# Weight spectra: the row transform of a 64x64 plane as products on the two row halves of TensorE, with copies of two PSUM banks

## The chip, the cores and the metric

One NeuronCore of a Trainium2 chip runs the whole program in one launch. The metric is the device time of that launch in microseconds (us), the median of several runs. All inputs and outputs are float32 in HBM.

## The reference, cut to what matters

The input `x` (16 images, 32 channels, 64x64 pixels) goes through four layers; each adds a convolution of its group-normalised input to `x`. The change concerns the fourth, which convolves with 32x32 filters of 64x64 pixels through Fourier transforms:

```python
x_f = jnp.fft.rfft2(x)
k_f = jnp.fft.rfft2(weights)          # weights: (32, 32, 64, 64)
out_f = jnp.einsum('bchw,ochw->bohw', x_f, k_f)
out = jnp.fft.irfft2(out_f, s=(H, W))
```

`k_f`, the weight spectra, depend on no other layer. The kernel computes them first of all, in a stage of its own, and keeps them in HBM until the fourth layer.

## The kernel before, in words

**The tiles.** `kernel_spectra_stage` (L270) goes over 8 tiles, in a loop of 4 rounds with two tiles each (`p` = 0 and 1, with their own source buffers `ks_src`). A tile has 128 planes of 64x64 pixels on the 128 partitions, 4096 pixels each: 8 chunks of 512.

**The steps of a tile.** All four are TensorE work in float32, written out in `forward_products` (L361).

1. `turn(j)` (L373) transposes chunk j, four blocks of 128x128 against the identity (L378), into PSUM bank `j % 4`. VectorE copies the bank to `ks_tt`, one of four buffers (L435, in `copy_turned`). A block of 128 turned partitions holds two image rows of 64 pixels, one in partitions 0 to 63, one in 64 to 127.
2. `rows(j)` (L381) is the transform along the rows: four products (L385), each with a 128x128 block of `ks_tt` as stationary operand (loaded into the array by a weight load) and the constant `ks_fw` as moving operand. `ks_fw` is block diagonal: twice the same 64x64 matrix, zeros elsewhere, so half of each product multiplies by zero. The result goes to bank `4 + j % 4`. ScalarE copies each bank back over `ks_src` (L447, in `copy_rows`).
3. `turn_columns(s)` (L398) transposes again (L404), into banks 0 to 3, which VectorE copies to `ks_cols` (L438). In odd tiles VectorE takes statistics of `x` in between (L204).
4. `columns(s)` (L407) is the transform along the columns (L412); for s = 0 four products more with 32 columns of weights (L417). ScalarE copies the results to `ks_spec` (L352), which its queue then sends to HBM (L357).

**What sets the order.** The order on TensorE is written out: three chunks are turned ahead (`AHEAD`), then turn(j+3) and rows(j) alternate, for j = 5 to 7 only rows are left; the columns go the same way. TensorE's queue waits for `turned_read` (VectorE has copied a turned bank) and `made_read` (ScalarE has emptied a result bank); the first `turn_columns` waits for all row copies of the tile, since it reads pixels of every chunk. VectorE waits for `turned` and, from chunk 4 on, for `made`, because the buffer `ks_tt` of chunk j-4 must have been used by its row product. `made` counts 16 per tile: 8 chunks and 8 column steps. SyncE's queue loads the next tiles (L303) and `x` (L305), two tiles ahead.

A float32 product runs as two weight loads and two matmul instructions, so that the 256 row products are 512 records of each kind; a transpose is one of each.

Of the kernel before, what the change touches and what calls it, by code (L numbers as in the profile page):

```python
# [19 lines left out]
F32 = mybir.dt.float32  # L20
# [7 lines left out]
P = 128  # L28
# [127 lines left out]
class Program:  # L156


    def __init__(self, nc, ctx, ins, out):
        self.nc, self.ins, self.out, self.names = nc, ins, out, set()  # L160
        self.ctx = ctx
        self.X = self.sb(ctx, "X", [P, Q, PIX])
        self.ident = self.sb(ctx, "ident", [P, P])
        self.pair = self.sb(ctx, "pair", [P, P])
        self.bn = self.sb(ctx, "bn", [P, NCH, 6])
        self.mv = self.sb(ctx, "mv", [P, 2])
        self.st = self.sb(ctx, "st", [P, Q, 2])
        self.gm = self.sb(ctx, "gm", [P, Q, 2])
        self.var = self.sb(ctx, "var", [P, Q])
        self.sd = self.sb(ctx, "sd", [P, Q])  # L170
        self.rstd = self.sb(ctx, "rstd", [P, Q])
        self.shift = self.sb(ctx, "shift", [P, Q])
        self.eps = self.sb(ctx, "eps", [P, 2])
        self.psum = [ctx.enter_context(nc.psum_tensor(f"bank{i}", [P, CH], F32)) for i in range(8)]
        self.zero = self.sb(ctx, "zero", [P, 1])


        self.pace = self.sem("pace")
        self.kf = nc.dram_tensor("kf", (SLOT // 4, P, 2, C // IB, IB * N), F32, kind="Internal").ap()
        self.kf_stored = self.sem("kf_stored")  # L180
        self.xf = nc.dram_tensor("xf", (Q, 2, C, KT, KX * 2 * IB), F32, kind="Internal").ap()
# [88 lines left out]
def kernel_spectra_stage(pr, loads, filt):  # L270

    nc, ps = pr.nc, pr.psum
    tiles = C // IB
    const, loaded = pr.sem("ks_const"), [[pr.sem(f"ks_load{p}{k}") for k in range(4)] for p in range(2)]
    x_loaded, layer_const = pr.sem("ks_x"), pr.sem("ks_layer_const")
    turned, turned_read = pr.sem("ks_turned"), pr.sem("ks_turned_read")
    made, made_read = pr.sem("ks_made"), pr.sem("ks_made_read")  # L280
    stored, step, eps = pr.kf_stored, pr.sem("ks_step"), pr.sem("ks_eps")
    w_tiles = pr.ins["L3_conv_weights"].rearrange("(t o) c h w -> t (o c) (h w)", o=IB)
    x_groups = pr.ins["x"].rearrange("(q b) c h w -> q (b c) (h w)", b=IB)
    with ExitStack() as ctx:

        spec = pr.sb(ctx, "ks_spec", [P, SLOT // 4, 2, IB, N])
        src = [pr.sb(ctx, f"ks_src{p}", [P, PIX]) for p in range(2)]
        tt = [pr.sb(ctx, f"ks_tt{p}", [P, CH]) for p in range(4)]
        cols = pr.sb(ctx, "ks_cols", [P, IB, SLOT, C])
        fw, fh, fh0 = (pr.sb(ctx, f"ks_{n}", [P, P]) for n in ("fw", "fh", "fh0"))  # L290
        with nc.Block() as block:
            @block.sync
            def _(sp):
                for t, n in ((pr.ident, "ident"), (pr.pair, "pair"), (fw, "l3_fw"), (fh, "l3_fh"), (fh0, "l3_fh0")):
                    sp.dma_start(t[:], pr.ins[n]).then_inc(const, 16)
                sp.sem_inc(x_loaded, START)
                with sp.Fori(0, tiles // 2) as i:
                    for p in range(2):

                        sp.wait_ge(turned, START + 32 * i + 16 * p - 16)  # L300
                        for k in range(4):
                            at = slice(k * PIX // 4, (k + 1) * PIX // 4)
                            sp.dma_start(src[p][:, at], w_tiles[2 * i + p][:, at]).then_inc(loaded[p][k], 16)  # L303
                    sp.wait_ge(x_loaded, 16 * i + START)
                    sp.dma_start(pr.X[:, i, :], x_groups[i]).then_inc(x_loaded, 16)  # L305
                filt.load(sp)
                for t, n in loads:
                    sp.dma_start(t[:], pr.ins[n]).then_inc(layer_const, 16)
                sp.wait_ge(layer_const, 16 * len(loads))

            @block.tensor
            def _(pe):

                pe.sem_inc(turned, START)
                pe.wait_ge(const, 16 * 5)
                with pe.Fori(0, tiles // 2) as i:
                    for p in range(2):
                        forward_products(pe, pr, src[p], tt, cols, fw, fh, fh0, 32 * i + 16 * p,
                                         turned, turned_read, made, made_read,
                                         lambda j: pe.wait_ge(loaded[p][j // 2], 16 * i + 16))  # L320

            @block.vector
            def _(dve):
                dve.memset(pr.eps[:], GN_EPS).then_inc(eps, 1)
                dve.memset(pr.zero[:], 0.0).then_inc(eps, 1)
                filt.clear(dve)
                with dve.Fori(0, tiles // 2) as i:
                    for p in range(2):
                        def stats(s):

                            if p == 1:
                                if s == 0:
                                    dve.wait_ge(x_loaded, START + 16 * i + 16)
                                pr.chunk_stats(dve, i, s, step)

                        copy_turned(dve, ps, tt, cols, 32 * i + 16 * p, turned, turned_read, made, stats)
                    pr.group_stats(dve, i, step)
                filt.find_largest(dve)

            @block.scalar  # L340
            def _(act):
                act.sem_inc(made_read, START)
                act.sem_inc(stored, START)
                with act.Fori(0, tiles // 2) as i:
                    for p in range(2):
                        base = 32 * i + 16 * p
                        copy_rows(act, ps, src[p], base, made, made_read)
                        for s in range(SLOT // 4):
                            act.wait_ge(made, base + NCH + s + 1)
                            if s == 0:  # L350
                                act.wait_ge(stored, START + 64 * i + 32 * p)
                            act.copy(spec[:, s].rearrange("p r o k -> p o r k"),  # L352
                                     ps[4 + s % 4][:].rearrange("p (o r k) -> p o r k", o=IB, r=2)
                                     ).then_inc(made_read, 1)
                        act.wait_ge(made_read, START + base + 16)
                        for part in range(2):
                            act.dma_start(pr.kf[:, :, part, 2 * i + p, :].rearrange("s p n -> p s n"),  # L357
                                          spec[:, :, part].rearrange("p s o k -> p s (o k)")).then_inc(stored, 16)


def forward_products(pe, pr, src, tt, cols, fw, fh, fh0, base, turned, turned_read, made, made_read,  # L361
                     src_ready):


# [4 lines left out]


    ps = pr.psum

    def turn(j):  # L373
        src_ready(j)
# [4 lines left out]
        m.then_inc(turned, 1)  # L379

    def rows(j):  # L381
        pe.wait_ge(turned_read, base + j + 1)
        pe.wait_ge(made_read, START + base + j - 3)
        for k in range(4):
            m = pe.matmul(ps[4 + j % 4][:, k * P:(k + 1) * P], tt[j % 4][:, k * P:(k + 1) * P], fw[:],  # L385
                          start=True, stop=True)
        m.then_inc(made, 1)

    AHEAD = 3
    for j in range(AHEAD):  # L390
        turn(j)
    for j in range(NCH):
        if j + AHEAD < NCH:
            turn(j + AHEAD)
        rows(j)
    spectra = src[:].rearrange("p (k s) -> p k s", s=SLOT)

    def turn_columns(s):  # L398
        if s == 0:
            pe.wait_ge(made_read, START + base + NCH)  # L400
        if s >= 4:
            pe.wait_ge(turned_read, base + NCH + s - 3)
        for k in range(4):
# [3 lines left out]
    def columns(s):  # L407
        pe.wait_ge(turned_read, base + NCH + s + 1)
        if s >= 4:
            pe.wait_ge(made_read, START + base + NCH + s - 3)  # L410
        for b in range(IB):
            m = pe.matmul(ps[4 + s % 4][:, b * P:(b + 1) * P],  # L412
                          cols[:, b, 4 * s:4 * s + 4].rearrange("p s c -> p (s c)"),
# [12 lines left out]
        columns(s)  # L426


def copy_turned(dve, ps, tt, cols, base, turned, turned_read, made, after=lambda s: None):

    for j in range(NCH):
        dve.wait_ge(turned, START + base + j + 1)
        if j >= 4:
            dve.wait_ge(made, base + j - 3)
        dve.tensor_copy(tt[j % 4][:], ps[j % 4][:]).then_inc(turned_read, 1)  # L435
    for s in range(SLOT // 4):
        dve.wait_ge(turned, START + base + NCH + s + 1)
# [2 lines left out]
        after(s)  # L440


def copy_rows(act, ps, src, base, made, made_read, after=lambda j: None):

    for j in range(NCH):
        act.wait_ge(made, base + j + 1)
        act.copy(src[:, j * CH:(j + 1) * CH], ps[4 + j % 4][:]).then_inc(made_read, 1)  # L447
        after(j)

# [1209 lines left out]
```

## Time and profile before

| what | value |
|---|---|
| median of 3 runs | 1067.43 us |
| lowest and highest run | 1066.34 and 1069.4 us |
| span of the profiled execution, first to last instruction | 1065.9 us |
| TensorE matmul busy | 907.4 us, 85% |
| TensorE weight load busy | 764.7 us, 72% |
| VectorE, ScalarE, GpSimd busy | 663.4, 520.5, 122.4 us |
| the stage of the change | from 8.0 us to about 201 us |

The profile gives only the span of its own execution; that lies 0.4 us under the lowest run and 1.5 us under the median. PE is the matmul side of TensorE and PEld its weight-load side; both can be busy together. A duration of one matmul record is its latency through the array and not its share of the time: in a dense stream the starts lie closer together. So the rate is read from a stretch, as (length of the stretch minus one record) over (records minus one). PEclk is the granted clock as a share of 2.4 GHz.

### The profile page before, as it was taken

The numbers are of one execution on the slowest core, as the hardware profiler recorded it, in microseconds if no ns is written. First come the engines' busy times: TensorE is split into PE (matmuls) and PEld (weight loads), VectorE is DVE, ScalarE is ACT, GpSimd is POOL, SyncE is SP. The second block draws the span as 40 slices with busy tenths as digits, with TensorE's granted clock in tenths as the row PEclk, the third lists the DMA queues.
The fourth block names the chain that finished last, engine by engine and source line by source line (L and its number), as shares of the span: only waits on it lengthen the run. The fifth ranks groups of instructions, "written<-read, shape, count | busy, mean of one in ns | idle before, by whom it ended". The sixth has DMA issues, their size and how long they took to land. (4 is left out here: it accounts for less than half of the span.)

```text
span 1065.9 us, 25662 instructions
## 1 busy us (share of the span) xinstructions
PE 907.4 (85%) x9335; PEld 764.7 (72%) x9335; DVE 663.4 (62%) x1208; ACT 520.5 (49%) x900; POOL 122.4 (11%) x120
## 2 busy tenths in 40 slices
PE   6999999876449956599789999995888699998998
PEld 6999999765348843499644444443887699998998
DVE  3556463765584769578778565756666688881232
ACT  2444444575344436255369997000888423225554
POOL 0000000010001016155401223000000100001110
PEclk9999999898679989699999999997999899999999
DMA  6465766464300000000000000001300337750222
GB/s 249 159 243 195 272 216 202 129 147 94 76 4 1 0 14 1 0 1 0 0 2 1 0 0 0 0 0 29 66 0 0 79 82 146 145 103 1 89 108 118
DMA packets 47673, 79.12 MB, mean 74 GB/s; under 512 B 19322, under 2 KB 37888, under 8 KB 44816
## 3 DMA queue, kind: packets, MB, share of 16 engines
q1 hardware_dynamic: 30992, 61.80, 20.9%
q10 hardware_dynamic: 16640, 16.78, 4.5%
q8 instruction: 26, 0.43, 0.2%
q14 instruction: 15, 0.12, 0.0%
HBM read 50.65 MB, written 27.92 MB: 74 GB/s over the span
## 5 line engine op out<-in xcount | busy, mean ns | idle before, releaser
L1436 DVE SCALAR_TENSOR_TENSOR X<-bank,c_power,X 32x512 f32 x128 | 95.8, 748 | 58.8 <-PE bank L1404 53.6
L1561 PE MATMUL bank<-m_xp,m_kf 128*32 128x64 f32 x2048 | 116.5, 224 | 6.8 <-DVE m_xp L1529 5.4
L1561 PEld LDWEIGHTS bank<-m_xp,m_kf 128*32 128x32 f32 x2048 | 116.2, 139 | 7.2 <-issue 7.2
L1404 PE MATMUL bank<-c_rh,c_w_high 128*128 x288 | 110.3, 383 | 3.3 <-DVE c_rl L1349 3.3
L1404 PE MATMUL bank<-c_rl,c_w_high 128*128 x288 | 110.2, 383 | 0.0
L1404 PE MATMUL bank<-c_rh,c_w_low 128*128 x288 | 110.2, 383 | 0.0
L923 DVE TENSOR_TENSOR X<-X,bank 128x512 f32 x64 | 43.6, 682 | 91.6 <-PE bank L909 91.6
L204 DVE BATCH_NORM_STATS2 bn<-X 128x6 f32 x128 | 85.6, 684 | 2.4 <-POOL X L1208 1.6
L1577 ACT COPY xm<-bank 64x512 f32 x64 | 32.5, 584 | 95.4 <-PE bank L1561 95.4
L1363 ACT ACTIVATE c_r<-X,c_nrm 32x1024 f32 (+1 forms) x56 | 73.6, 1314 | 2.4 <-DVE c_nrm L1412 1.1
L438 DVE COPY ks_cols<-bank 128x512 f32<-128x512 f32 x64 | 42.6, 682 | 45.9 <-PE bank L404 45.9
L435 DVE COPY ks_tt<-bank 128x512 f32<-128x512 f32 x64 | 42.3, 688 | 44.1 <-PE bank L378 44.1
L352 ACT COPY ks_spec<-bank 128x512 f32<-128x512 f32 x64 | 37.4, 587 | 65.4 <-PE bank L412 29.1
L1161 PE MATMUL bank<-mm,p_tt 128*128 128x128 f32 x512 | 63.0, 278 | 3.1 <-DVE X L1191 3.1
L385 PE MATMUL bank<-ks_fw,ks_tt 128*128 128x128 f32 x512 | 64.6, 277 | 0.0
L412 PE MATMUL bank<-ks_fh,ks_cols 128*128 128x128 f32 x512 | 63.7, 275 | 0.0
L1161 PEld LDWEIGHTS bank<-mm,p_tt 128*128 128x128 f32 x512 | 59.9, 193 | 4.8 <-DVE X L1191 4.5
L385 PEld LDWEIGHTS bank<-ks_fw,ks_tt 128*128 128x128 f32 x512 | 61.3, 194 | 0.0
L447 ACT COPY ks_src<-bank 128x512 f32<-128x512 f32 x64 | 37.2, 587 | 48.4 <-PE bank L385 48.4
L412 PEld LDWEIGHTS bank<-ks_fh,ks_cols 128*128 128x128 f32 x512 | 60.4, 192 | 0.0
L909 PE MATMUL bank<-c_l_iw,i_tt 128*128 128x128 f32 (+1 forms) x384 | 60.1, 310 | 0.0
L626 DVE TENSOR_TENSOR f_tl<-bank,f_th 128x512 f16<-128x512 f32 x64 | 42.3, 683 | 26.1 <-ACT f_th L581 25.9
(187 smaller groups left out, 1951.7 us busy)
## 6 DMA issues: line engine op xcount, KB each, us to landing
ks_src<-in_L_conv_weights SPq DMA_DIRECT2D x32, 512.0 KB, 6.3
kf<-ks_spec ACTq DMA_DIRECT2D x16, 1024.0 KB, 10.0
m_kf<-kf SPq DMA_DIRECT2D x32, 512.0 KB, 8.0
X<-in_x SPq DMA_DIRECT2D x4, 2048.0 KB, 12.3
out_y<-X SPq DMA_DIRECT2D x16, 512.0 KB, 2.7
xf<-f_xm SPq DMA_DIRECT2D x6, 448.0 KB
l_wb<-in_L_conv_weights_r SPq DMA_DIRECT2D x4, 512.0 KB, 13.1
l_wb<-in_L_conv_weights_i SPq DMA_DIRECT2D x4, 512.0 KB, 14.7
```

The lines of the kernel that those rows point to most:

```text
L204: dve.bn_stats(self.bn[:, c, :], self.X[:, q, c * CH:(c + 1) * CH]).then_inc(step, 1)
L385: m = pe.matmul(ps[4 + j % 4][:, k * P:(k + 1) * P], tt[j % 4][:, k * P:(k + 1) * P], fw[:], start=True, stop=True)
L412: m = pe.matmul(ps[4 + s % 4][:, b * P:(b + 1) * P], cols[:, b, 4 * s:4 * s + 4].rearrange("p s c -> p (s c)"), fh[:], start=True, stop=True)
L435: dve.tensor_copy(tt[j % 4][:], ps[j % 4][:]).then_inc(turned_read, 1)
L438: dve.tensor_copy(cols[:, :, 4 * s:4 * s + 4].rearrange("p b s c -> p s b c"), ps[s % 4][:].rearrange("p (s b c) -> p s b c", s=4, b=IB)). ...
L909: m = pe.matmul(ps[4 + c % 4][:, k * n:(k + 1) * n], tt[g % 4][:, (first + k) * P:(first + k + 1) * P], mw[:], start=True, stop=True)
L923: dve.tensor_tensor(x, x, ps[4 + c % 4][:], ALU.add).then_inc(added, 1)
L1161: m = pe.matmul(ps[2 + 2 * (j % 2) + t][:, k * P:(k + 1) * P], tt[j % 2][:, k * P:(k + 1) * P], mm[:, t, :], start=True, stop=True)
L1363: act.activation(to, of, ACT.Identity, scale=nrm[at, 0, bass.ds(q, 1)], bias=nrm[at, 1, bass.ds(q, 1)]).then_inc(ready[b], 1)
L1404: m = pe.matmul(ps[n][:], w[:, ky, kx].rearrange("p o c -> p (o c)"), d[:, q, b, y:y + HALF, x:x + HN], start=i == 0, stop=i == len(terms) ...
L1436: dve.scalar_tensor_tensor(x, ps[n][o * C:(o + 1) * C, :].rearrange("p (y x) -> p y x", x=HN), filt.power[at, 2:3], x, ALU.mult, ALU.add). ...
L1561: last = pe.matmul(ps[4 * half + m // 8][at:at + C, m % 8 * N:(m % 8 + 1) * N], kf[p][:, j, :, H * half + m], xp[half][:, j, m].rearrange( ...
```

## The change

The row transform no longer multiplies by the block diagonal 128x128 matrix. Each block of `ks_tt` is used in two products: partitions 0 to 63 with the upper 64x64 block of `ks_fw`, and partitions 64 to 127 with the lower one. The first writes into the even bank of a pair, the second into the odd one. Two chunks make one row step, of 16 products; there are four steps (`ROW_STEPS`) in place of eight. ScalarE copies both banks of a pair with one instruction of 1024 elements per partition, which puts the two halves back into pixel order. For that the eight PSUM banks are one tensor. Before row step j, TensorE now turns chunks 2j+3 and 2j+4. `made` counts 12 per tile. The other steps, the loads and the stores are as before.

```diff
+        self.banks = ctx.enter_context(nc.psum_tensor("bank", [P, 8, CH], F32))
+        self.psum = [self.banks[:, i] for i in range(8)]
...
+ROW_STEPS = NCH // 2
+MADE = ROW_STEPS + SLOT // 4
...
     def rows(j):
-        pe.wait_ge(turned_read, base + j + 1)
-        pe.wait_ge(made_read, START + base + j - 3)
-        for k in range(4):
-            m = pe.matmul(ps[4 + j % 4][:, k * P:(k + 1) * P], tt[j % 4][:, k * P:(k + 1) * P], fw[:],
-                          start=True, stop=True)
+        pe.wait_ge(turned_read, base + 2 * j + 2)
+        pe.wait_ge(made_read, START + first + (2 * j - 2 if j < 2 else j - 1))
+        for k in range(8):
+            for h in range(2):
+                at = slice(h * N, (h + 1) * N)
+                m = pe.matmul(ps[4 + 2 * (j % 2) + h][:, k * N:(k + 1) * N],
+                              tt[(2 * j + k // 4) % 4][at, k % 4 * P:(k % 4 + 1) * P], fw[at, at], start=True, stop=True)
         m.then_inc(made, 1)
...
-    for j in range(NCH):
-        if j + AHEAD < NCH:
-            turn(j + AHEAD)
+    for j in range(ROW_STEPS):
+        for ahead in (2 * j + AHEAD, 2 * j + AHEAD + 1):
+            if ahead < NCH:
+                turn(ahead)
         rows(j)
...
         if j >= 4:
-            dve.wait_ge(made, base + j - 3)
+            dve.wait_ge(made, MADE * tile + j // 2 - 1)
         dve.tensor_copy(tt[j % 4][:], ps[j % 4][:]).then_inc(turned_read, 1)
...
-    for j in range(NCH):
-        act.wait_ge(made, base + j + 1)
-        act.copy(src[:, j * CH:(j + 1) * CH], ps[4 + j % 4][:]).then_inc(made_read, 1)
-        after(j)
+    for j in range(ROW_STEPS):
+        act.wait_ge(made, MADE * tile + j + 1)
+        act.copy(src[:, 2 * j * CH:2 * (j + 1) * CH].rearrange("p (k h n) -> p k h n", h=2, n=N),
+                 pr.banks[:, 4 + 2 * (j % 2):6 + 2 * (j % 2)].rearrange("p h (k n) -> p k h n", n=N)).then_inc(made_read, 1)
```

## Rows read from the trace of the kernel before

**Rows 1.** The page: engines' busy time, and TensorE's slices of the span

```profile
PE 907.4 (85%) x9335; PEld 764.7 (72%) x9335; DVE 663.4 (62%) x1208; ACT 520.5 (49%) x900; POOL 122.4 (11%) x120
...
PE   6999999876449956599789999995888699998998
```

**Rows 2.** Windows: PE, PEld, DVE, ACT, POOL busy, granted clock, DMA share, GB/s; the stage

```profile
8.00:201.20 193.20, 185.52 (x1600) 181.27 (x1601) 105.69 (x173) 78.48 (x132) 0.00 (x0) 1.00 0.59 206
```

**Rows 3.** Waits, all engines, 8 to 202 us: us in total, times, longest

```profile
ACT ks_src L447 <- PE bank L385: 48.4, 58, 11.1
DVE ks_cols L438 <- PE bank L404: 45.9, 24, 4.2
DVE ks_tt L435 <- PE bank L378: 44.1, 43, 6.9
...
PE bank L404 <- ACT ks_src L447: 5.4, 8, 0.7
```

**Rows 4.** Groups by line and shape, 0 to 330 us: busy us, mean ns, idle before

```profile
L385 PE MATMUL bank<-ks_fw,ks_tt 128*128 128x128 f32 x512 | 64.6, 277 | 0.0
...
L385 PEld LDWEIGHTS bank<-ks_fw,ks_tt 128*128 128x128 f32 x512 | 61.3, 194 | 0.0
```

**Rows 5.** Timeline of tile 2, end of the row transform: start, length, instructions

```profile
40.95 0.47 PEld L378 LDWEIGHTS bank<-ident,ks_src 128*128 128x128 f32 x4
41.06 0.60 PE L378 MATMUL bank<-ident,ks_src 128*128 128x128 f32 x4
...
41.49 3.74 PE L385 MATMUL bank<-ks_fw,ks_tt 128*128 128x128 f32 x32
...
45.27 0.59 ACT L447 COPY ks_src<-bank 128x512 f32<-128x512 f32 x1 [0.31 <-PE bank L385]
45.91 1.86 PEld L404 LDWEIGHTS bank<-ident,ks_src 128*128 128x128 f32 x16 [0.87 <-ACT ks_src L447]
```

**Rows 6.** Timelines: weight loads of 128 columns before short moving operands, and of 16

```profile
201.19 0.30 PEld L236 LDWEIGHTS bank<-st,pair 128*128 128x128 f32 x2 [2.43 <-issue]
...
443.74 1.77 PEld L1041 LDWEIGHTS bank<-e_eb,c_l_spread 16*128 16x128 f32 x8 [1.87 <-DVE e_eb L1120]
443.74 1.96 PE L1041 MATMUL bank<-e_eb,c_l_spread 16*128 16x64 f32 x8 [1.78 <-DVE e_eb L1120]
```

**Rows 7.** Windows, columns as in rows 2, around the weight loads of rows 6

```profile
200.00:201.60 1.60, 0.36 (x2) 0.30 (x2) 0.00 (x0) 0.42 (x1) 0.00 (x0) 1.00 0.55 198
442.00:446.00 4.00, 1.96 (x8) 1.77 (x8) 1.60 (x8) 0.00 (x0) 0.00 (x0) 0.50 0.00 0
```

**Rows 8.** Groups by shape, whole span: 64 moving columns, 32 columns of weights

```profile
L1561 PE MATMUL bank<-m_xp,m_kf 128*32 128x64 f32 x2048 | 116.5, 224 | 6.8 <-DVE m_xp L1529 5.4 <-DVE m_xp L1515 1.4
```

**Rows 9.** Window and timeline: products on 64 rows and 32 columns, both row halves

```profile
289.40:293.20 3.80, 3.67 (x207) 3.63 (x208) 3.68 (x9) 0.00 (x0) 0.00 (x0) 0.50 0.02 4
...
289.48 3.67 PE L762 MATMUL bank<-l_xb,l_wb 64*32 64x32 f32 x207 [13.79 <-DMA l_xb<-xf]
```

**Rows 10.** Timeline of tile 2: into the 32-column products of L417 and out

```profile
47.80 1.06 PE L412 MATMUL bank<-ks_fh,ks_cols 128*128 128x128 f32 x8
...
48.78 0.79 PEld L417 LDWEIGHTS bank<-ks_fh,ks_cols 128*32 128x32 f32 x8
48.78 1.06 PE L417 MATMUL bank<-ks_fh,ks_cols 128*32 128x128 f32 x8
...
49.77 0.52 PEld L404 LDWEIGHTS bank<-ident,ks_src 128*128 128x128 f32 x4 [0.20 <-DVE ks_cols L438]
49.78 0.71 PE L404 MATMUL bank<-ident,ks_src 128*128 128x128 f32 x4
```

**Rows 11.** Timeline: from products with 64 columns of weights to 128 columns

```profile
337.18 1.91 PE L866 MATMUL bank<-ident,i_yq 128*64 128x128 f32 x16
338.93 3.74 PE L882 MATMUL bank<-c_l_ih,i_cols 128*128 128x128 f32 x32
```

**Rows 12.** Groups by shape, 0 to 330 us: ScalarE's copies from PSUM

```profile
L447 ACT COPY ks_src<-bank 128x512 f32<-128x512 f32 x64 | 37.2, 587 | 48.4 <-PE bank L385 48.4
...
L772 ACT COPY l_y<-bank 32x256 f32<-32x256 f32 x16 | 5.8, 365 | 0.2
```

**Rows 13.** Timeline of tile 3, its begin: VectorE's four copies in a row

```profile
58.55 2.48 DVE L435 COPY ks_tt<-bank 128x512 f32<-128x512 f32 x4 [1.25 <-PE bank L378]
```

**Rows 14.** Timeline of tile 1 under the half clock: eight row product records

```profile
11.27 1.83 PEld L385 LDWEIGHTS bank<-ks_fw,ks_tt 128*128 128x128 f32 x8
```

**Rows 15.** Timeline of a later stage: the same 16 transposes under the half clock

```profile
320.15 3.60 PE L866 MATMUL bank<-ident,i_yq 128*64 128x128 f32 x16 [5.58 <-DVE i_yq L840]
```

More of the change, by code:

```diff
@@ L173, in __init__ @@
         self.eps = self.sb(ctx, "eps", [P, 2])
-        self.psum = [ctx.enter_context(nc.psum_tensor(f"bank{i}", [P, CH], F32)) for i in range(8)]
+        self.banks = ctx.enter_context(nc.psum_tensor("bank", [P, 8, CH], F32))
+        self.psum = [self.banks[:, i] for i in range(8)]
         self.zero = self.sb(ctx, "zero", [P, 1])
@@ L334, in stats @@
                                 pr.chunk_stats(dve, i, s, step)
-                        copy_turned(dve, ps, tt, cols, 32 * i + 16 * p, turned, turned_read, made, stats)
+                        copy_turned(dve, ps, tt, cols, 2 * i + p, turned, turned_read, made, stats)
                     pr.group_stats(dve, i, step)
@@ L345, in _ @@
                     for p in range(2):
-                        base = 32 * i + 16 * p
-                        copy_rows(act, ps, src[p], base, made, made_read)
+                        first = MADE * (2 * i + p)
+                        copy_rows(act, pr, src[p], 2 * i + p, made, made_read)
                         for s in range(SLOT // 4):
-                            act.wait_ge(made, base + NCH + s + 1)
+                            act.wait_ge(made, first + ROW_STEPS + s + 1)
                             if s == 0:
@@ L354, in _ @@
                                      ).then_inc(made_read, 1)
-                        act.wait_ge(made_read, START + base + 16)
+                        act.wait_ge(made_read, START + first + MADE)
                         for part in range(2):
@@ L358, in _, with forward_products @@
                                           spec[:, :, part].rearrange("p s o k -> p s (o k)")).then_inc(stored, 16)
-def forward_products(pe, pr, src, tt, cols, fw, fh, fh0, base, turned, turned_read, made, made_read,
+ROW_STEPS = NCH // 2
+MADE = ROW_STEPS + SLOT // 4
+def forward_products(pe, pr, src, tt, cols, fw, fh, fh0, tile, turned, turned_read, made, made_read,
                      src_ready):
     ps = pr.psum
+    first = MADE * tile
+    base = 2 * NCH * tile
     def turn(j):
@@ L399, in turn_columns @@
         if s == 0:
-            pe.wait_ge(made_read, START + base + NCH)
+            pe.wait_ge(made_read, START + first + ROW_STEPS)
         if s >= 4:
@@ L409, in columns @@
         if s >= 4:
-            pe.wait_ge(made_read, START + base + NCH + s - 3)
+            pe.wait_ge(made_read, START + first + ROW_STEPS + s - 3)
         for b in range(IB):
@@ L426, in forward_products, with copy_turned @@
         columns(s)
-def copy_turned(dve, ps, tt, cols, base, turned, turned_read, made, after=lambda s: None):
+def copy_turned(dve, ps, tt, cols, tile, turned, turned_read, made, after=lambda s: None):
+    base = 2 * NCH * tile
     for j in range(NCH):
@@ L440, in copy_turned, with copy_rows @@
         after(s)
-def copy_rows(act, ps, src, base, made, made_read, after=lambda j: None):
-    for j in range(NCH):
-        act.wait_ge(made, base + j + 1)
-        act.copy(src[:, j * CH:(j + 1) * CH], ps[4 + j % 4][:]).then_inc(made_read, 1)
-        after(j)
+def copy_rows(act, pr, src, tile, made, made_read):
+    for j in range(ROW_STEPS):
+        act.wait_ge(made, MADE * tile + j + 1)
+        act.copy(src[:, 2 * j * CH:2 * (j + 1) * CH].rearrange("p (k h n) -> p k h n", h=2, n=N),
+                 pr.banks[:, 4 + 2 * (j % 2):6 + 2 * (j % 2)].rearrange("p h (k n) -> p k h n", n=N)).then_inc(made_read, 1)
 class Forward:
```

2 lines of the change are left out of this document (1 added, 1 removed).

## The prediction

> **What bounds the kernel now.** I read the page first: TensorE is busy for 85% of the span, and its slices stand at 9 through the first seven, where the weight spectra are made [rows 1]. The window of this stage says it more sharply: in 193.2 us the matmul side is busy 185.5 us, the weight-load side 181.3 us, VectorE 105.7 and ScalarE 78.5, at the full clock (2.4 GHz) [rows 2]. The waits confirm it from the other side: ScalarE and VectorE wait for TensorE (48.4, 45.9 and 44.1 us), and TensorE waits for an engine in one place only, before the first column transpose of each tile, eight times, 5.4 us in all, until ScalarE has copied the last row result [rows 3]. So whatever TensorE gains or loses here goes to the end of the program; the next stage starts with TensorE's last result.
>
> The row products are 512 matmul records [rows 4]. Their rate stands in the timeline: 32 of them take 3.74 us, which less one record of 0.277 and over 31 is **112 ns each**; 512 make 57.3 us. The four transposes before them run at (0.60 - 0.28) / 3 = 107 to 110 ns [rows 5]. The question is which side of TensorE sets the 112 ns, since the change halves only one of them.
>
> **The products themselves.** Per block of 128x128 the change streams 64 columns in place of 128, twice, on 64 rows each. It does not shorten the weight load: a stationary operand of 64 rows still has 128 columns, and there are 1024 loads in place of 512. What does a load of 128 float32 columns cost with next to nothing to stream behind it? Two loads with 8 moving columns take 0.30 us; less one load of 0.19 that is 0.11 us between starts, at the full clock. With 16 rows and 64 moving columns, eight take 1.77 us, (1.77 - 0.33) / 7 = 0.206 us, at the half clock, so 0.103 at the full one [rows 6, 7]. Fewer rows do not make it shorter, and fewer moving columns don't either. So loads take **108 ns** each (I take the row at the full clock, between 103 and 112), and the present 112 ns are bound by loads and matmuls alike. Shortening the stream alone gains only 4 ns per instruction.
>
> The Trainium skill, "TensorE: Matmul & The Clock Gate", section "LDWEIGHTS (loading the stationary operand)", speaks against this change: a load's time goes with its columns, and 32 rows take as long as 128. The rows agree, with 16 rows as above; its formula would give 107 ns, and by it the sum would be the same within 1 us.
>
> What remains is that the two halves work side by side. The trace has products on both row halves in turn, of 64 rows and 32 columns: 207 records in 3.67 us, 17 ns each, at the half clock. The rate of one tile at the half clock would be about 57 ns: L1561's 2048 records with twice the moving columns take 116.5 us, 57 ns, at twice the clock [rows 8, 9]. Three to four such products, loads included, thus run side by side. They differ in columns as well as in rows, so that this does not prove it for halves that both use all 128 columns. I take it as full: 16 loads per half and row step at 108 ns, and the second half one load behind, since loads start in the order of the queue. A row step then takes 17 x 0.108 = 1.84 us from its first load to the start of its last product; before, its 16 records took 16 x 0.112 = 1.79.
>
> **Changing between whole and half array.** New are the changes between transposes (all 128 rows) and row products (64 rows). The nearest rows are the four L417 products with 32 columns. The last L412 record before them starts at 47.80 + 1.06 - 0.275 = 48.59, the first L417 load and matmul only at 48.78: 0.20 us where 0.11 is usual, and no load was brought forward. Back: last L417 at 48.78 + 1.06 - 0.27 = 49.57, next at 49.78, again 0.20, and the four transposes take 0.71 and not 0.60, their first load of 128 columns lying open [rows 5, 10]. The other end: from 64 columns of weights to 128 nothing is lost, 337.18 + 16 x 0.11 = 338.93 [rows 11].
> The Trainium skill, "TensorEngine Tiling (Array Packing)", section "Key Properties", says that a change of tiling mode drains TensorE. The rows of L417 agree (0.09 us each way besides the open load), those of L866 show no drain; by the rule the sum is the one below, without it the second rival.
> I take the L417 price, since the row halves are a tiling as the 32 columns are. Counted from the last transpose's start to the next transpose's start: before 0.11 + 1.79 = 1.90 us; after 0.20 (drain) + 1.84 + 0.15 (drain, 0.05 less as 64 columns stream) + 0.11 (open load) = 2.30. That is +0.40 for each of the steps 0 and 1. Steps 2 and 3 have only the turn of chunk 7 ahead of them and follow one another: 0.20 + 33 x 0.108 + 0.05 = 3.81 to the end of the last product, before 0.11 + 32 x 0.112 = 3.69, so +0.12. The way out of it is hidden in the wait for ScalarE. Per tile 0.92 us.
>
> **The copies.** ScalarE's copy of 256 elements takes 365 ns, of 512 587 ns: 0.87 ns per element [rows 12]. One of 1024 is then 1.03 us. Bounds: 0.59 (if the second bank came free) and 1.17 (two old ones). The rest of them is hidden: one per step of about 2.7 us with its turns. The last is not: the first column transpose waits for it, 0.87 us behind the last row product now [rows 5], **+0.44 us** per tile. It costs nothing else: queued behind ScalarE's wait are only its own copies and, a tile later, the stores.
>
> **Waits and order.** Row step 0 needs chunks 0 and 1; VectorE's four copies go at 0.60 to 0.69 us each [rows 13], done while turns 3 and 4 run: nothing. VectorE's copy of chunk 4 now waits for the whole of row step 0, and chunk 5 behind it too; step 2 needs both. Between lie turns 5 and 6 (0.88 us) and step 1 (2 us), against 1.3 us plus 0.2 of latency: covered. Chunks 6 and 7 wait for step 1 and are covered by turn 7 and step 2, 2.3 us. If a step took half its time this cover would be 1.4 us and 0.1 to 0.2 us would open. SyncE's loads hang on `turned`, which moves by less than a us per tile and has a whole tile of cover; in the first tile turn 4 needs the third quarter of the source ahead of row step 0, at most a few tenths once. Chunks two ahead on `made_read` leave a whole step. No cost for the single PSUM tensor: banks and addresses stay.
>
> **The sum.** 8 x (0.92 + 0.44) = **+10.9 us** on a span of 1065.9: 1076.8. The runs' median lies 1.5 us above the span, so 1078.4.
>
> **The rivals.**
> *No drain* (as rows 11 show for 64 columns). Per single step 17 x 0.108 + 0.06 = 1.90, as before; steps 2 and 3 gain 0.08; the copy costs 0.44: 8 x 0.36 = +2.9, **1070.3**. For it: L866. Against: L417. Chance 25%.
> *The halves' loads do not overlap*, since both need all columns. Then 1024 loads at 108 ns, 110.6 us against 57.3: +53 us, less the stagger, plus drains and copy: **about 1130**. Against: rows 9 as far as they go. 8%.
> *Faster: a load on half the rows takes less*, so that only the stream counts: 57 ns per record [rows 8], two side by side, 16 x 0.057 = 0.91 us per step in place of 1.79, 32 times: -28 us, +11 for drains and copies: **1050**. It decides as soon as a load takes under 88 ns, where 17 x 20 ns pays for the 0.34 us per step (10.9 us over 32). Against it: 16 rows at 103 [rows 6]. 10%.
> The Trainium skill, the same tiling page, section "Theoretical Speedup", allows up to 2x for 64 rows; that is this rival, and rows 6 stand against it.
> *The clock falls* because less of the array streams: a record then takes (1.83 - 0.2) / 7, 0.22 to 0.23 us, twice 112 ns [rows 14]; only in the row steps that is +57 us. The window of rows 9 stood at the half clock, but between pauses. 2%. That the change does not do what it says can be left out: it is plain in the diff.
>
> **How the numbers follow.** Forecast 55%, the likeliest, 1078.4. About 0.3% or 3.2 us is what a measurement of this kernel can tell from no change. Bounds of the forecast: loads at 112 ns add 0.004 x 67 x 8 = 2.1 us, a copy of 1.17 us adds 1.1, a change of mode that costs 0.1 more adds 0.1 x 5 x 8 = 4; a stage later that meets the half clock or leaves it moves 2 us either way (16 transposes 3.60 against 1.91 us [rows 11, 15]). High end 1088. Low end: no drain (1070.3), the copy for nothing (-3.5) and the clock (-2): 1064. This holds the two first cases, 80%. Within 0.3% lies most of the no-drain case, 20%; slower are the forecast, the serial loads, the clock and a sliver of no drain, 69%; faster 11%.
>
> **What would show it.** Right: 1024 L385 loads of 64x128 still at 108 ns per half (54 between starts), a step of 1.8 us; 0.2 us between the last transpose and the first half load; 0.87 us before L404 grown to 1.3; ScalarE copies of about 1.03 us; clock 1.00 in the stage; the stage 11 us longer, the rest as before. Wrong: a step under 1.5 us (faster loads) or near 3.5 (serial); loads brought forward across the change (no drain); VectorE's wait for `made` showing up as a TensorE wait for `ks_tt`.

## The result and the profile after

The changed kernel takes 1083.72 us in the median (1081.71 to 1089.53, 4 runs), the kernel before 1068.41 us in the runs beside it. The ratio is **1.015** (95% interval 1.0118 to 1.0183): slower by 15 us, forecast +11 us and 1078.4. The profiled execution has a span of 1082.0 us, against 1065.9.

The engines' line of the changed kernel's page, and groups by shape from 0 to 220 us: the row products and ScalarE's new copy. As in all rows below, the line numbers are the kernel's own: L385 turns, L395 row products, L415 column transposes, L423 column products, L459 row copies.

```profile
PE 922.0 (85%) x9847; PEld 773.1 (71%) x9847; DVE 662.9 (61%) x1208; ACT 515.5 (48%) x868; POOL 122.3 (11%) x120
...
L395 PE MATMUL bank<-ks_fw,ks_tt 64*128 64x64 f32 x1024 | 62.8, 275 | 0.0
L395 PEld LDWEIGHTS bank<-ks_fw,ks_tt 64*128 64x128 f32 x1024 | 59.4, 189 | 4.2 <-issue 4.2
...
L459 ACT COPY ks_src<-bank 128x1024 f32<-128x1024 f32 x32 | 32.4, 1012 | 61.2 <-PE bank L395 61.2
```

Half as much streaming, and the row products keep TensorE as busy as before (62.8 us; 64.6 in [rows 4]). The small matmul that opens the next stage starts at 201.19 us in [rows 6]; in the timeline of the changed kernel:

```profile
216.38 0.30 PEld L237 LDWEIGHTS bank<-st,pair 128*128 128x128 f32 x2 [2.42 <-issue]
```

So 15.2 of the span's 16.1 us lie in the stage of the change. The timeline of its second tile, which answers to [rows 5]:

```profile
36.56 2.35 PE L385 MATMUL bank<-ident,ks_src 128*128 128x128 f32 x20
...
38.84 1.86 PEld L395 LDWEIGHTS bank<-ks_fw,ks_tt 64*128 64x128 f32 x32 [0.17 <-issue]
38.84 2.00 PE L395 MATMUL bank<-ks_fw,ks_tt 64*128 64x64 f32 x32
40.77 0.86 PEld L385 LDWEIGHTS bank<-ident,ks_src 128*128 128x128 f32 x8
40.77 1.09 PE L385 MATMUL bank<-ident,ks_src 128*128 128x128 f32 x8
...
43.73 0.66 PE L385 MATMUL bank<-ident,ks_src 128*128 128x128 f32 x4
...
44.31 3.79 PE L395 MATMUL bank<-ks_fw,ks_tt 64*128 64x64 f32 x64
...
49.21 1.86 PEld L415 LDWEIGHTS bank<-ident,ks_src 128*128 128x128 f32 x16 [1.25 <-ACT ks_src L459]
```

The last transpose starts at 36.56 + 2.35 - 0.27 = 38.64, the first half load 0.20 later (the drain); the 32 records of a step need 2.00 - 0.27 = 1.73 us from first to last start, 111 to 112 ns for each pair; the next load comes 0.20 after the last start; and the eight transposes take 0.06 more than 7 x 0.109 + 0.27. Together 2.19 us where it was 1.90: **+0.29** for each of the steps 0 and 1. Steps 2 and 3: from 44.12 to 48.10, 3.98 us; in [rows 5] from 41.39 to 45.23, 3.84: **+0.14**. Then come the waits before the column transposes; on the matmul side, from the end of the last product, the changed kernel's is 1.11 us (its line is shown below) and that of the kernel before 0.68:

```profile
45.91 2.05 PE L404 MATMUL bank<-ident,ks_src 128*128 128x128 f32 x16 [0.68 <-ACT ks_src L447]
```

That is **+0.43**. Per tile these make 1.15 us. The tiles as a whole say the same: where the clock stands, the first column transpose of a tile follows that of the tile before by 24.65 us, and by 23.48 in the kernel before, 1.17 more:

```profile
100.14 2.06 PE L415 MATMUL bank<-ident,ks_src 128*128 128x128 f32 x16 [1.11 <-ACT ks_src L459]
...
124.79 2.06 PE L415 MATMUL bank<-ident,ks_src 128*128 128x128 f32 x16 [1.11 <-ACT ks_src L459]
```

The first tile reaches its column transposes only 0.5 us later than before (22.94 against 22.43 us), in part since its source arrived 0.3 us earlier. So 0.5 and seven times 1.17 make 8.7 of the 15.2 us. That is the forecast's mechanism, and it leaves 6.5.

The rest is the clock. Windows of the changed kernel (columns: us, PE, PEld, DVE, ACT, POOL busy, granted clock, DMA share, GB/s):

```profile
23.20:26.80 3.60, 3.60 (x20) 3.60 (x20) 2.42 (x4) 0.00 (x0) 0.00 (x0) 0.53 0.00 0
74.40:78.00 3.60, 3.60 (x20) 3.60 (x19) 2.76 (x4) 0.00 (x0) 0.00 (x0) 0.53 0.51 180
149.50:153.00 3.50, 3.50 (x17) 3.50 (x18) 2.41 (x5) 0.00 (x0) 0.00 (x0) 0.51 0.00 0
78.00:149.50 71.50, 68.16 (x773) 64.88 (x772) 33.52 (x55) 27.50 (x37) 0.00 (x0) 1.00 0.60 205
```

And its timeline, the column transposes of the first and of the second tile:

```profile
22.94 3.48 PE L415 MATMUL bank<-ident,ks_src 128*128 128x128 f32 x16 [1.11 <-ACT ks_src L459]
...
49.21 2.06 PE L415 MATMUL bank<-ident,ks_src 128*128 128x128 f32 x16 [1.11 <-ACT ks_src L459]
```

In three tiles (and in the eighth, at 201 us) TensorE drops to 1.2 GHz as it comes out of the wait for ScalarE, and the same 16 transposes take 3.48 in place of 2.06 us. From them to the first L428 product it is 4.50 us in place of 2.88, so each fall costs 1.62 us, four of them 6.5. In [rows 2] the window reads 1.00 for the whole stage. Both kernels do run their first 5 us at the half clock, as the length of their records shows [rows 14], though windows there read 1.00; behind that the kernel before has no fall in the stage.

### The profile page after: what moved, and what is told of

It reads as the page before. It is cut to its first block and busy times, and to the rows that moved or that the text cites. A ratio compares the mean times of both kernels' runs of the same rounds, so it can differ in the third digit from the quotient of the medians.

```text
span 1082.0 us, 26574 instructions
## 1 busy us (share of the span) xinstructions
PE 922.0 (85%) x9847; PEld 773.1 (71%) x9847; DVE 662.9 (61%) x1208; ACT 515.5 (48%) x868; POOL 122.3 (11%) x120
## 5 line engine op out<-in xcount | busy, mean ns | idle before, releaser
L423 PE MATMUL bank<-ks_fh,ks_cols 128*128 128x128 f32 x512 | 64.8, 278 | 0.0
L395 PE MATMUL bank<-ks_fw,ks_tt 64*128 64x64 f32 x1024 | 62.8, 275 | 0.0
L395 PEld LDWEIGHTS bank<-ks_fw,ks_tt 64*128 64x128 f32 x1024 | 59.4, 189 | 4.2 <-issue 4.2
L423 PEld LDWEIGHTS bank<-ks_fh,ks_cols 128*128 128x128 f32 x512 | 61.9, 196 | 0.0
L459 ACT COPY ks_src<-bank 128x1024 f32<-128x1024 f32 x32 | 32.4, 1012 | 61.2 <-PE bank L395 61.2
L1525 DVE COPY m_xp<-xm 32x1024 f32 (+1 forms) x64 | 45.4, 709 | 22.4 <-PE bank L1573 18.5
## 6 DMA issues: line engine op xcount, KB each, us to landing
l_wb<-in_L_conv_weights_i SPq DMA_DIRECT2D x4, 512.0 KB, 15.2
```

The lines of the kernel that those rows point to most:

```text
L395: m = pe.matmul(ps[4 + 2 * (j % 2) + h][:, k * N:(k + 1) * N], tt[(2 * j + k // 4) % 4][at, k % 4 * P:(k % 4 + 1) * P], fw[at, at], start= ...
L423: m = pe.matmul(ps[4 + s % 4][:, b * P:(b + 1) * P], cols[:, b, 4 * s:4 * s + 4].rearrange("p s c -> p (s c)"), fh[:], start=True, stop=True)
L1525: dve.tensor_copy(re, of.rearrange("p k r b -> p k (r b)"))
```

## The experiments

Each is an edit of the changed kernel. A stage's end is the start of the small matmul behind it: 201.2 us before, 216.4 changed. A tile's period is the time from the first column transpose of the fourth tile to that of the fifth, where the clock stands at 1.00: 23.48 us before, 24.65 changed.

**The longer copy and the step of two chunks alone.**

The row products are whole again; the copy (not shown) puts its two banks back in their order.

```diff
         for k in range(8):
-            for h in range(2):
-                at = slice(h * N, (h + 1) * N)
-                m = pe.matmul(ps[4 + 2 * (j % 2) + h][:, k * N:(k + 1) * N], ..., fw[at, at], ...)
+            m = pe.matmul(ps[4 + 2 * (j % 2) + k // 4][:, k % 4 * P:(k % 4 + 1) * P],
+                          tt[(2 * j + k // 4) % 4][:, k % 4 * P:(k % 4 + 1) * P], fw[:], start=True, stop=True)
```

> The row products are whole again (128 rows, 128 columns, eight per step), but two chunks still make one step with one copy of 1024 elements, and the order of the turns is that of the change. Nothing is left out. Theory: the longer copy alone costs 0.38 us per tile (the wait before the column transposes 1.25 us in place of 0.87), 3 us in all, and if that wait is what makes the clock fall, the clock falls here too, once or more in the stage, for another 1.7 us each: 1071 to 1078 us, granted clock under 1.00 in the stage. Rival: the clock fell because half products keep less of the array busy; then the clock stays at 1.00 through the stage and the time is 1071 us.

Ratio 1.004 (1.002 to 1.006), median 1074.2 us, stage end 203.9 us. Its timeline shows the wait at full length:

```profile
46.03 1.86 PEld L413 LDWEIGHTS bank<-ident,ks_src 128*128 128x128 f32 x16 [1.29 <-ACT ks_src L457]
```

Its window (PE busy, granted clock, DMA share, GB/s) shows no fall:

```profile
8.00:203.00 195.00, 184.81 (x1600) 1.00 0.58 203
```

The copy costs 0.43 us in each tile (its period is 23.91), 2.7 at the stage's end, where the theory had 3. The clock did not fall here behind the same wait: the theory was wrong on that. The median lies 4.5 us above the kernel before (its interval is 2 to 6 us), more than the stage shows; the rest lies in later stages and was not followed up.

**All turns of a tile first.**

```diff
-    for j in range(AHEAD):
+    for j in range(NCH):
         turn(j)
     for j in range(ROW_STEPS):
-        for ahead in (2 * j + AHEAD, 2 * j + AHEAD + 1):
-            if ahead < NCH:
-                turn(ahead)
         rows(j)
```

> The changed kernel, but all eight chunks of a tile are turned before row step 0, so that the four row steps follow one another: one change into the half array per tile in place of three. Nothing is left out. Theory (each pass from transposes to half products and back costs 0.29 us): 2 x 0.29 x 8 = 4.6 us less than the changed kernel, 1079 us, with the wait before the column transposes unchanged at 1.25 us, and the clock still falling. Rival: the passes cost nothing and only the second half's late start and the copies do; then the time stays within 1 us of the changed kernel. Rival: the early turns make VectorE late for step 2 and TensorE waits for a turned chunk; then 1.3 us per tile are lost, +10 us.

Median 1077.95 us, ratio to the kernel before 1.0105 (1.0056 to 1.0154), stage end 210.0 with two falls of the clock, at 47.6 and 170.5 us. The tile's period is 24.23 us, 0.42 under the changed kernel, where twice 0.29 was expected. The rest is a new wait of the turns for VectorE, 0.18 us in seven of the eight tiles:

```profile
63.76 0.42 PEld L385 LDWEIGHTS bank<-ident,ks_src 128*128 128x128 f32 x4 [0.18 <-DVE ks_tt L444]
64.34 7.22 PEld L395 LDWEIGHTS bank<-ks_fw,ks_tt 64*128 64x128 f32 x128 [0.17 <-issue]
```

With it the two passes fewer per tile are worth 0.60 us, 0.30 each, and the changed kernel's timeline gave 0.29. The intervals of the totals overlap those of the changed kernel; the stage's timeline carries this verdict.

**The last row step copied by two engines.**

```diff
+    dve.wait_ge(made, MADE * tile + ROW_STEPS)
+    dve.tensor_copy(src[:, 6 * CH:].rearrange("p (k h n) -> p k h n", h=2, n=N)[:, :, 1],
+                    ps[7].rearrange("p (k n) -> p k n", n=N)).then_inc(pr.shared, 1)
...
+        n = 1 if j == ROW_STEPS - 1 else 2
+        act.copy(src[...].rearrange("p (k h n) -> p k h n", h=2, n=N)[:, :, 0:n],
+                 pr.banks[:, 4 + 2 * (j % 2):4 + n + 2 * (j % 2)].rearrange("p h (k n) -> p k h n", n=N)
+                 ).then_inc(made_read, 1)
```

TensorE waits for both copies before the column transposes.

> The changed kernel, but of the last row step of a tile ScalarE copies the even bank and VectorE the odd one, at the same time. Nothing is left out. Theory: the wait before the column transposes falls from 1.25 to 0.9 us (a copy of 0.69 in place of 1.01), 2.6 us in all; and as the clock fell only right behind this wait, it no longer falls in the stage, another 4 x 1.7 = 6.8 us: 1074 to 1075 us with clock 1.00 in the stage. Rival (the clock falls because half products keep less of the array busy): 1081 us, with as many falls.

Median 1080.49 us (ratio 1.0116, 1.0084 to 1.0149), stage end 210.7. The wait fell to 0.93 us, but the clock still fell twice, here right behind a wait of 0.80 us on the matmul side, which is little more than the 0.68 us of the kernel before. The timeline of the second tile:

```profile
47.00 3.62 PE L418 MATMUL bank<-ident,ks_src 128*128 128x128 f32 x16 [0.80 <-DVE ks_src L452]
```

And the window there (PE busy, granted clock, DMA share, GB/s):

```profile
47.20:50.60 3.40, 3.40 (x17) 0.50 0.02 5
```

The tile's period is 24.33 us, 0.32 under the changed kernel: the copy's share as expected, 2.6 us in eight tiles. The clock was expected to stay up and fell twice, where the rival had as many falls as in the changed kernel. The wait's length alone is not what decides.

**Both together.** The two edits above.

> Both together: all eight turns first, and the last row step copied by ScalarE and VectorE side by side. Nothing is left out. Theory: 1083.7 - 4.6 - 2.6 - 6.8 = 1070 us, clock 1.00 in the stage, still not under the kernel before, since the loads of 128 columns keep a row step at 1.8 us. Rival (loads on half the array leave room that the pauses had hidden): under 1066 us.

Median 1075.28 us, ratio 1.0063 (1.0031 to 1.0094), 5 us above the 1070 expected. The profiled execution, at 1072.13 us one of the two fastest, has no fall in the stage and ends it at 204.2 us, 3.0 us behind the kernel before. Its clock was 0.949 in the mean and that of the four other executions 0.932 to 0.940, so they may have had falls in it. The tile's period is 23.91 us, 0.43 above the kernel before: half products, their passes and copies cut down as far as these edits go, still lose.

**All 128 columns streamed on each half.** The second chunk's blocks overwrite those of the first, so half the row results are lost; the loads are those of the change.

```diff
-                m = pe.matmul(ps[4 + 2 * (j % 2) + h][:, k * N:(k + 1) * N], ..., fw[at, at], ...)
+                m = pe.matmul(ps[4 + 2 * (j % 2) + h][:, k % 4 * P:(k % 4 + 1) * P], ..., fw[at, :], ...)
```

> The changed kernel, but each half product streams all 128 columns of the constant, so that it takes twice the stream on its 64 rows; the blocks of the second chunk of a step overwrite those of the first, so half the row results are lost. Loads and their number stay. Theory (loads set the pace): a row step stays at 1.8 us (112 ns per record and half, as loads of 128 columns and streams of 128 take the same), only the last product streams 0.05 us longer: time within 3 us of the changed kernel. Rival (the stream sets it): 3.5 us per step, +55 us. As to the clock: if it fell because little of the array streams, it stays at 1.00 now in spite of the same wait of 1.25 us; if the wait alone makes it fall, it falls as before.

One run, 1076.77 us, stage end 211.8. Twice the stream, and a row step is only 0.06 us longer, as its timeline shows:

```profile
37.93 2.06 PE L395 MATMUL bank<-ks_fw,ks_tt 64*128 64x128 f32 x32
```

Its window (columns as in the last one):

```profile
8.00:211.00 203.00, 192.61 (x2112) 1.00 0.56 195
```

So streams of up to 128 columns hide behind these loads: the **loads set the pace** of a row step. And the clock did not fall, although the wait was that of the changed kernel (1.11 us on the matmul side). That is one execution; so both kernels ran once more.

> The changed kernel itself, for a second profile and to be compared on one chip with the three others. Theory: the stage again has several short stretches at the half clock, 1.7 us lost in each, right behind the wait before the column transposes (or across it): 1080 to 1086 us. Rival (their place and number are chance): none in the stage, 1076 us.

> The half products with all 128 columns streamed (half the row results are lost) once more, timed in rounds beside the changed kernel. Theory (the clock falls when little of the array streams before and after the wait): no fall in the stage, and the kernel that streams twice as much is faster than the changed one by 4 to 7 us, 1076 to 1079 us. Rival (one lucky profile): the same time as the changed kernel or 1 to 2 us more.

The changed kernel: 1087.5 us, a little over the 1080 to 1086 expected, ratio 1.0173 (1.0143 to 1.0203), with falls at the same four places, here three of them as windows (PE busy, granted clock, DMA share, GB/s):

```profile
23.60:27.00 3.40, 3.40 (x19) 0.50 0.00 0
74.80:78.20 3.40, 3.40 (x18) 0.50 0.50 179
149.90:153.30 3.40, 3.40 (x18) 0.50 0.00 0
```

The wide one: 1083.01 us where 1076 to 1079 were expected, ratio 1.0117 (1.0079 to 1.0156), again without any:

```profile
8.00:211.00 203.00, 191.97 (x2112) 1.00 0.56 196
```

Its stage ends at 211.1 us, 5.5 us before the changed kernel's 216.6, although its steps are longer. The falls do not come at random: they hit the same four tiles in both profiles of the changed kernel and none in both of the wide one, which differs only in the columns that it streams and waits as long. Behind the whole products of the first experiment the same wait left the clock up too, in one profile. What the runs do not show is why four of the changed kernel's eight tiles are hit and four, with the same products and the same 1.11 us, are not. Something besides the products before the wait has a part in it, so a single profile without a fall (the first experiment, both edits together) is weaker evidence than the two of the wide kernel. In the total the gain is 4.5 us between the medians, and the two intervals overlap.

**Upper halves first, lower halves after.**

```diff
-        for k in range(8):
-            for h in range(2):
+        for h in range(2):
+            for k in range(8):
```

> The changed kernel, but the eight products on the upper half of a row step come first and the eight on the lower half after them, in place of in turn. Nothing is left out. Theory (loads and matmuls start in the order of the queue, and a half waits for its own weights): halves work side by side only where they alternate; now each half runs alone, a row step takes 32 x 0.108 = 3.5 us, +53 us in all, 1137 us. Rival (the queue brings loads and matmuls of the other half forward far enough): the step stays at 1.8 us.

One run, 1183.72 us, where 1137 was expected. Its timeline, a row step of the first tile and then the second tile:

```profile
12.54 6.29 PE L395 MATMUL bank<-ks_fw,ks_tt 64*128 64x64 f32 x32
...
54.42 2.35 PE L385 MATMUL bank<-ident,ks_src 128*128 128x128 f32 x20
56.69 3.39 PE L395 MATMUL bank<-ks_fw,ks_tt 64*128 64x64 f32 x32
...
64.94 11.43 PE L395 MATMUL bank<-ks_fw,ks_tt 64*128 64x64 f32 x64
```

The windows in the fall and before it (PE, PEld, DVE, ACT, POOL busy, granted clock, DMA share, GB/s):

```profile
65.20:82.00 16.80, 15.70 (x85) 15.51 (x85) 3.92 (x7) 2.30 (x3) 0.00 (x0) 0.50 0.01 4
44.70:65.00 20.30, 20.30 (x183) 19.34 (x182) 7.35 (x12) 6.25 (x10) 0.00 (x0) 1.00 0.62 205
```

At the full clock a step takes 3.39 us in place of 2.00: with 16 records on one half before the 16 on the other, the halves hardly work side by side. It also settles what a load costs. The wide kernel alone would fit loads of 54 ns, one after the other; but here one half alone has (3.39 - 0.27) / 31 = 0.10 us between starts with only 64 columns to stream. The stream does not add to that, since in the wide kernel twice the stream hid behind the loads; so a load on 64 rows takes about 0.10 us. The step's +1.39 us is 45 us in 32 of them. The rest of the 100 us is the clock, which now falls in seven of eight tiles, here in the middle of the row products with no pause before it, and stays down for 14 to 17 us: steps 2 and 3 take 11.43 us where 3.79 stood. The first tile never left the half clock before 44 us: its step took 6.29 us. TensorE was busy throughout (20.30 of 20.30 us) when it fell, with one half of the array at a time.

**Four tiles of 64 rows and 64 columns.** If the loads set the pace and go with their columns, cut their columns:

```diff
+        pe.sem_inc(pr.pace, 1)
         for k in range(8):
-            for h in range(2):
-                at = slice(h * N, (h + 1) * N)
-                m = pe.matmul(ps[4 + 2 * (j % 2) + h][:, k * N:(k + 1) * N],
-                              tt[...][at, k % 4 * P:(k % 4 + 1) * P], fw[at, at], ...)
+            for c in range(2):
+                for h in range(2):
+                    at, to = slice(h * N, (h + 1) * N), slice(c * N, (c + 1) * N)
+                    m = pe.matmul(ps[4 + 2 * (j % 2) + h][to, k * N:(k + 1) * N],
+                                  tt[...][at, k % 4 * P + c * N:k % 4 * P + (c + 1) * N], fw[at, at], ...)
```

Nothing waits for the semaphore `pace`; this kernel and the three after it count it up once per step, and what that costs was not measured by itself.

> The changed kernel, but each half product is cut once more, into two with 64 columns of weights each: four tiles of 64 rows and 64 columns take turns, 32 products per row step in place of 16. Nothing is left out. Theory (loads of 128 columns set the 1.8 us of a row step, since a load goes with its columns): a load now takes 54 ns and a stream 57, four tiles side by side make 14 ns between starts, or 17 if the starts themselves are the limit as in the products of rows 9: a step of 64 records takes 0.9 to 1.1 us in place of 1.84, 32 steps gain 24 to 30 us less what VectorE's copies then hold up: 1056 to 1064 us. Rival (something else than the loads sets the pace, such as 56 ns per record start on the array or in the queue): twice as many records, a step of 3.6 us, 1140 us. Rival (column tiles of the same rows don't run side by side): 1.8 us, 1083 us.

Median 1061.54 us, ratio **0.9942** (0.9919 to 0.9964): faster than the kernel before, by half a per cent. A step's 64 records, the same work as the changed kernel's 32, in the timeline of the second tile:

```profile
39.56 1.16 PE L397 MATMUL bank<-ks_fw,ks_tt 64*64 64x64 f32 x64
40.65 1.09 PE L385 MATMUL bank<-ident,ks_src 128*128 128x128 f32 x8
```

(1.16 - 0.22) / 63 = 15 ns between starts; 0.94 us where 1.73 stood. A new cost shows in its timeline of the first tile:

```profile
20.48 2.33 PE L397 MATMUL bank<-ks_fw,ks_tt 64*64 64x64 f32 x73 [2.67 <-issue]
```

TensorE pauses with nothing to wait for that the profile shows, 2.67 us here and 2.24 in the second tile, and the clock is down around each pause for some 7 us. It happens only the first time that each of the two unrolled tiles is run; what it is was not tried. It takes most of the gain: from the third tile to the seventh the period is 21.43 or 21.44 us, 3.2 under the changed kernel and 2.0 under the kernel before, but the two periods from the first tile to the third are 6.3 us longer together, and the first pause comes ahead of them. The clock stays up behind the wait for ScalarE, 1.12 us here, in the third to the eighth tile.

**The same, and the last step split, with turns in three orders.** All eight turns first:

> Four tiles as in the run before, all eight turns of a tile ahead of row step 0, and the last row step copied by ScalarE and VectorE side by side. Nothing is left out. Theory: the row steps, 1.1 us each, outrun VectorE now: it copies chunks 4 and 5 (1.3 us) only after step 0, 6 and 7 only after step 1, so steps 2 and 3 wait together 0.5 to 0.8 us per tile, 5 us in all, against 4.6 us from the changes of mode and 2.6 from the split: 1052 to 1062 us, about as the run before or 2 to 3 us less. Rival (VectorE keeps up, since its copies overlap the turns as before): 1050 us or less.

Median 1059.64 us (0.9943, 0.9915 to 0.997), stage end 195.5. Now VectorE is late, as expected, in every tile; the third in the timeline:

```profile
66.72 2.10 PE L399 MATMUL bank<-ks_fw,ks_tt 64*64 64x64 f32 x128
69.48 2.36 PE L399 MATMUL bank<-ks_fw,ks_tt 64*64 64x64 f32 x128 [0.66 <-DVE ks_tt L450]
```

Its tile's period is 21.68 us, above the 21.43 of the four tiles alone, though a part of the last copy went to VectorE here.

The turns as in the change:

> Four tiles of 64x64, turns as in the change, the last row step copied by ScalarE and VectorE side by side. Nothing is left out. Theory: 2.6 us less than the four tiles alone (1061.5 us) by the shorter wait, 1059 us. Rival: the wait does not set the end here, 1061.5 us.

Median **1053.66 us**, ratio **0.9847** (0.9825 to 0.987), the fastest measured; stage end 192.3 us. The timeline of tile 4, at the full clock:

```profile
88.33 1.16 PE L399 MATMUL bank<-ks_fw,ks_tt 64*64 64x64 f32 x64
89.43 0.66 PE L387 MATMUL bank<-ident,ks_src 128*128 128x128 f32 x4
90.01 2.24 PE L399 MATMUL bank<-ks_fw,ks_tt 64*64 64x64 f32 x128
93.06 2.06 PE L421 MATMUL bank<-ident,ks_src 128*128 128x128 f32 x16 [0.81 <-DVE ks_src L455]
```

Against the four tiles alone that is 8 us where 2.6 were expected, and 10 us when each is set against the kernel before that ran beside it. The stage gained 2.6 (194.9 to 192.3; the period 0.32, to 21.11), so the rest lies in later stages or between the two samples, and is not settled. Chunks 0 to 5 turned before steps 0 and 1, 6 and 7 before steps 2 and 3:

> As the run before, but chunks 0 to 5 are turned before row steps 0 and 1, chunks 6 and 7 before steps 2 and 3: two changes into the tiles per tile of weights in place of three, and VectorE has time for every chunk. Nothing is left out. Theory: 0.29 us per tile less than the run before, and none of the 0.65 us that all turns first cost (TensorE's wait for a turned chunk before step 2): 1057 us, the fastest of all. Rival: the waits for VectorE come back, 1060 us.

Median 1056.19 us (0.9888, 0.9853 to 0.9924), stage end 190.9. The total is near the 1057 expected, and not to be told apart from the last one; the theory of it failed. A tile takes 21.12 us, no less than 21.11: in the timeline of the third tile steps 2 and 3 take 2.45 us where 2.29 stood there, with a pause of 0.23 us between their loads that names no wait. That uses up what the pass saved:

```profile
66.86 2.45 PE L399 MATMUL bank<-ks_fw,ks_tt 64*64 64x64 f32 x128
```

The 1.4 us by which the stage ends earlier lie in the first tile, whose column transposes start at 21.92 in place of 23.57 us.

## Why the prediction was right, and where it was short

*What bounds the stage, and that a loss there goes straight to the end.* Right: 15.2 of the 16.1 us lie in the stage.

*Loads of 128 columns set the pace.* Right: streams of 128 columns cost nothing more, one half alone starts a record only every 0.10 us, and with loads of 64 columns, four tiles in turn, the step halves. The load's 108 ns was slightly low in the step: the pairs come at 111 to 112 ns, as before.

*The halves side by side.* Right; rows 9, with differing columns, did carry over. The stagger of one load did not come: the loads of the two halves start within 0.01 us of each other. So a step is 1.73 us and not 1.84.

*The change of mode.* The price taken from the L417 products, 0.20 us to the first load, was exact on both sides; the way out was put at 0.26 with the open load and is 0.26. The way back in [rows 10] names a copy of VectorE before the load, so that it could have been a wait and no drain; in the changed kernel the same 0.20 us stand where nothing is named. With the stagger gone +0.40 became +0.29 per step. The Trainium skill, "TensorEngine Tiling (Array Packing)", "Key Properties", has the drain, and the trace agrees with its 0.20 us in place of 0.11. The rival without a drain fell, and so did the one of serial loads.

*The copy.* Forecast 1.03 us and +0.44 per tile, measured 1.012 and +0.43; alone it makes the tile's period 0.43 us longer.

*The rival on the other side* (loads shorter on fewer rows) fell: on 64 rows they have nearly the pace of 128. The Trainium skill, "TensorEngine Tiling (Array Packing)", section "Theoretical Speedup", has up to 2x for 64 rows. In this case that came only with 64 columns of weights as well: 1.73 to 0.94 us, 1.8x.

*The clock.* This is the term that was mis-sized. The forecast had it at nothing in its sum, as a rival of 2% with falls in the row steps, and 2 us either way from later stages. In fact it falls in four of eight tiles behind the row steps, at the wait, and costs 6.5 us in the stage; what picks the four is open.

*The total.* The mechanisms were put at 10.9 us and cost 8.7; with the clock's 6.5 that is the 15.2 measured. So the forecast of 1078.4 (its own terms give 1078.3) lies as near to 1083.72 as it does partly by luck: a stagger that did not come stood in for part of a clock that fell.

## What to carry to other kernels

Before halving what a product streams, ask what its weight load costs: here a float32 load of 128 columns took as long as 128 streamed columns (108 ns), so a half-height product with full-width weights gained nothing, while four 64x64 tiles in turn gave 1.8x on the step. The tiles ran side by side where consecutive products in the queue belonged to different tiles, and hardly where 16 records of one came before 16 of the other (3.39 us in place of 2.00). Each pass into tiled products and back cost 0.29 us, so put tiled products together, but only as far as the copying engines can follow: all eight turns first made the 64x64 kernel's tile 0.57 us longer. Where a stage runs at the full clock with small waits in it, look at the granted clock behind each of them in the new profile: here half products that stream 64 columns lost it behind a wait in four tiles of eight, and the same products streaming 128 did not.

## What the runs showed that was not expected

- The clock fell in a TensorE that was busy without a gap, when only one half of the array at a time took products of 64 columns: down for 14 to 17 us in seven of eight tiles, and not up before 44 us in the first.
- The same wait of 1.11 us left the clock at 1.00 behind whole products (one profile) and behind half products that stream 128 columns (two), and brought it to 0.50 in four of eight tiles behind half products that stream 64, at the same four places in two profiles.
- Streaming 64 more columns per product, of no use, made the kernel no slower: its stage was 4.6 and 5.5 us shorter, by the clock.
- Tiles of 64x64 in float32 start 15 ns apart.
- With 256 row product records in a tile in place of the changed kernel's 128, TensorE paused 2 to 3 us once in each of the two unrolled tiles, on their first pass; with the clock's falls around them these pauses cost more than the 6.3 us by which the stage got shorter.
